# First taps of two depthwise convolutions on ScalarE, split loads, new orders, no identity products

## The reference, cut to what matters

```python
# block L0: window attention (8x8 windows, 4 heads), gated 1x1, dense 3x3 convolution
x = x + proj(attention(x))
h = w1 @ x + w1_b;  a, b = split(h)
g = a * sigmoid(b);  g = replicate_pad(g)
x = x + leaky(conv3x3(g, w2) + w2_b)
# block L1: linear attention with rope
x = x + dwconv(x, cpe1)                       # depthwise 3x3
y = ln2d(x);  act = silu(act_proj @ y);  y = in_proj @ y
t = silu(dwconv(y, dwc_w) + dwc_b)            # depthwise 3x3, nine taps
q, k = elu(qk_w @ t) + 1;  v = t
kv = sum_n rope(k) * v;  z = 1 / (q . mean(k))
attn = rope(q) @ kv * z + dwconv(v, lepe_w) + lepe_b   # depthwise 3x3, nine taps
x = x + out_proj @ (attn * act)
x = x + dwconv(x, cpe2)
x = x + fc2 @ gelu(fc1 @ ln2d(x))
```

## Time and profile before

| | |
|---|---|
| median of 3 runs | 798.58 us (796.69 to 803.7) |
| the profiled execution | 797.02 us, span of the core 795.0 us |
| mean granted TensorE clock | 0.959 |
| PE busy | 732.6 us, 92% of the span |
| DVE busy | 533.7 us, 67% |
| ACT busy | 450.0 us, 57% |
| POOL busy | 309.4 us, 39% |
| identity products (line 837) | 444 matmuls, 57.2 us |
| ACT table loads (line 1023) | 53, 68.0 us |
| DMA | 9% to 10% of the 16 engines' span |

### The profile page before, as it was taken

One profiled execution on the slowest core, in us unless ns is written; L12 is line 12 of the kernel. 1 busy time (PEld: TensorE's weight loads), 2 busy tenths in 40 slices (PEclk: granted clock), 3 DMA queues, 4 the chain that ended last, 5 costly groups with the idle time before them and its releaser, 6 DMA issues.

```text
span 795.0 us, 19684 instructions
## 1 busy us (share of the span) xinstructions
PE 732.6 (92%) x8424; PEld 463.3 (58%) x8424; DVE 533.7 (67%) x677; ACT 450.0 (57%) x638; POOL 309.4 (39%) x230
## 2 busy tenths in 40 slices
...
GB/s 60 33 68 16 2 31 2 2 2 15 1 16 17 32 31 31 16 32 1 31 31 46 21 27 2 2 2 31 32 16 1 27 22 16 1 31 1 43 5 45
...
## 3 DMA queue, kind: packets, MB, share of 16 engines
...
q10 hardware_dynamic: 512, 0.04, 0.1%
...
## 4 chain that ended last, share of the span: by engine, by line
PE 58%; DVE 22%; issue 6%; POOL 5%; ACT 4%; SPq 4%; DMA 1%; ACTq 0%; DVEq 0%; POOLq 0%
PE ps L590 21%; DVE QS L1178 9%; PE ps L580 7%; PE ps L681 5%; PE ps L837 4%; DVE CT L1192 3%; PE ps L656 3%; PE ps L667 3%; PE ps L765 2%; SPq L468 2%; PE ps L810 2%; PE ps L827 2%; DVE SC L1122 1%; PE ps L635 1%; PE ps L644 1%
## 5 line engine op out<-in xcount | busy, mean ns | idle before, releaser
L1331 POOL TENSOR_TENSOR SC<-SC,mx 128x768 f32<-128x768 f32 x48 | 77.2, 1609 | 172.5 <-DVE mx L1126 172.5
L590 PE MATMUL ps<-XP,wdw 48*64 48x384 f32 x1728 | 144.0, 483 | 0.0
L1192 DVE SCALAR_TENSOR_TENSOR CT<-TP,vec_sb,CT 112x768 f32<-112x768 f32 x96 | 123.6, 1304 | 1.3
L590 PEld LDWEIGHTS ps<-XP,wdw 48*64 48x64 f32 x1728 | 68.1, 132 | 69.4 <-issue 56.6
L1178 DVE SCALAR_TENSOR_TENSOR QS<-XP,vec_sb,QS 112x768 f32<-112x768 f32 x96 | 104.8, 1133 | 0.5
L1122 DVE TENSOR_TENSOR SC<-ps,bias_sb 128x768 f32<-128x768 f32 x48 | 45.7, 953 | 54.6 <-PE ps L656 54.1
L590 PE MATMUL ps<-G,w_sb 48*64 48x384 f32 x864 | 73.8, 493 | 1.3 <-ACT QH L1018 1.3
L681 PEld LDWEIGHTS ps<-vx,PT 128*128 128x128 f32 x576 | 66.6, 192 | 9.0 <-issue 5.5
L681 PE MATMUL ps<-vx,PT 128*128 128x52 f32 x576 | 68.8, 275 | 0.8 <-DVE XP L1152 0.4
L1023 ACT ACT_TABLE_LOAD x53 | 68.0, 1283 | 0.9
L1336 POOL TENSOR_TENSOR XP<-XP,YB 112x768 f32<-112x768 f32 x12 | 22.4, 1870 | 110.2 <-DMA YB<-YF 110.2
...
## 6 DMA issues: line engine op xcount, KB each, us to landing
XP<-in_x_dram SPq DMA_DIRECT2D x48, 72.0 KB, 2.5
YB<-YF SPq DMA_DIRECT2D x48, 72.0 KB, 2.2
XP<-XB SPq DMA_DIRECT2D x48, 72.0 KB, 2.4
...
wln_sb<-in_const_dram SPq DMA_DIRECT2D x6, 9.0 KB
```

What stands on the lines that cost most here:

```text
L590: mm = pe.matmul(slot(job)[half(c, HALF), r * BANK:r * BANK + SPX], w[half(r), tap * HALF:(tap + 1) * HALF], shifted(t, d * CROWS + c * WI ...
L1192: dve.scalar_tensor_tensor(out=ct, in0=win, scalar=wt, in1=ct, op0=ALU.mult, op1=ALU.add).then_inc(lepe_step, 1)
L1331: pool.tensor_tensor(sc, sc, bc_last(mx[:, (u % NSC) * 12:(u % NSC) * 12 + 12], TOK), ALU.subtract).then_inc(sub_ready, 1)
```

## The change

Six things change.

1. The first taps `c10` and `c20` of both depthwise convolutions (12 jobs each) leave VectorE. ScalarE computes them as Identity activations with scale and bias. Two new semaphores, dwc_begun and lepe_begun, hand them to tap 1 on VectorE.
2. The 37 loads of loaded_b are split. 24 stay, 13 (`wout`, `swap`, `wfc2`, the rope tables, the masks) get a semaphore of their own, loaded_c, and are issued last. Only DVE job `z0` waits for loaded_c. Strips 3, 4 and 5 of pair 0 are issued among and behind the 24.
3. `kp` computes km_sb with a SCALAR_TENSOR_TENSOR, of the head mask times the PSUM scalar times the head mask. The factor 1/PX that the TENSOR_SCALAR applied goes into a column of eye2_sb, by one small VectorE instruction in `s2`.
4. All `+n` marks are gone from PE_ORDER, so no identity product is left.
5. All five orders and the PSUM slots are new. Counted from the new ACT_ORDER, there are 48 table loads. Among the large moves: `f1` and `f2` of pair 1, chunks 1 and 2 go 75 to 77 places forward in PE_ORDER, with their `ge` on ScalarE 72 to 75 and `o.1.1`, `o.1.2` on VectorE 51 and 60 places. `s3.0.0` goes 37 places back on PE, `v.3.0` to `v.3.2` 32 to 43. On VectorE `z0.0.0` now stands behind `s2.0.0`.
6. `s2` on VectorE waits for the set-up of GpSimd.

```diff
 PE_ORDER = """
...
-    q.3.2@0 kp.3.0@3+21 kk.3.0@2+7 dn.3.0@0 dn.3.1@1 dn.3.2@3 at.3.0@2+23 at.3.1@0+6 at.3.2@2+12 op.3.0@1+4
-    op.3.1@0+4 d3.3.0@3+31 op.3.2@2 xc2.3.0@1+2 va2.3.0@0+4 f12.3.0@3+14 f11.3.0@2 d3.3.1@1 d3.3.2@0 xc2.3.1@3
-    f10.3.0@2 xc2.3.2@1 va2.3.1@0 f2.3.0@3 va2.3.2@2 f12.3.1@1+9 f11.3.1@3 f10.3.1@0 f2.3.1@2+12 f12.3.2@1
-    f11.3.2@3 f10.3.2@0 f2.3.2@2+6
...
+    kv.3.1@2 q.3.0@0 q.3.1@1 q.3.2@3 kv.3.2@2 kp.3.0@0 kk.3.0@1 dn.3.0@3 dn.3.1@2 dn.3.2@0 at.3.0@1 at.3.1@3
+    at.3.2@1 op.3.0@2 op.3.1@3 d3.3.0@0 op.3.2@1 xc2.3.0@2 va2.3.0@3 f12.3.0@0 f11.3.0@1 f10.3.0@2 d3.3.1@3
+    f2.3.0@0 xc2.3.1@2 d3.3.2@1 va2.3.1@3 xc2.3.2@0 va2.3.2@2 f12.3.1@1 f11.3.1@3 f10.3.1@0 f2.3.1@2 f11.3.2@3
+    f12.3.2@0 f10.3.2@1 f2.3.2@2
...
+def begun(text, prefix):
+
+    found = [(i, n) for name, i, n in jobs(text) if name == prefix]
+    return {t: j + 1 for j, t in enumerate(found)}
...
+DWC_BEGUN, LEPE_BEGUN = begun(ACT_ORDER, "c10"), begun(ACT_ORDER, "c20")
...
-        N_V, N_QK, N_A, N_W, N_B = 2, 8, 6, 8, 37
+        N_V, N_QK, N_A, N_W, N_B, N_C = 2, 8, 6, 8, 24, 13
...
-            for t in range(3, STRIPS):
-                load(0, t)
             for b in range(2):
                 img = slice(b * C, (b + 1) * C)
-                load_b(wout_sb[half(b), 0:C], wsq3[img, 9, img])
...
                 load_b(eye2_sb[half(b, C + 1), :], ident[0:C + 1, 0:HALF])
+                load(0, 3 + b)
...
             load_b(fc1b_sb[:, :], fc1b)
+            load(0, STRIPS - 1)
+            for b in range(2):
+                img = slice(b * C, (b + 1) * C)
+                load_c(wout_sb[half(b), 0:C], wsq3[img, 9, img])
...
+            load_c(masks_sb[:, :], masks)
+            load_c(rope_th_sb[:, :], rope_th)
+            load_c(rope_tw_sb[:, :], rope_tw)
...
+                elif name == "c10":
+                    wait_read(act, ("ip", i, halo_last(n)))
+                    if i:
+                        wait_filled(act, ("at", i - 1, n))
+                    act.activation(rows16(T0[n]), shifted(XP[i % 2], n * CROWS, CROWS, TAPS[0])[0:RG], ACT.Identity,
+                                   scale=v(f"dwc_{TAPS[0]}"), bias=v("dwc_b")).then_inc(dwc_begun, 1)
+                elif name == "c20":
+                    act.wait_ge(t_ready, i * CH + halo_last(n) + 1)
+                    if kc >= 2:
+                        wait_filled(act, ("op", (kc - 2) // CH, (kc - 2) % CH))
+                    act.activation(rows16(CT[kc % 2]), shifted(TP, n * CROWS, CROWS, TAPS[0])[0:RG], ACT.Identity,
+                                   scale=v(f"lepe_{TAPS[0]}"), bias=v("lepe_b")).then_inc(lepe_begun, 1)
...
                 if name == "z0":
-                    dve.wait_ge(loaded_b, N_B * 16)
+                    dve.wait_ge(loaded_c, N_C * 16)
...
+                    dve.wait_ge(setup_pool, N_POOL)
+                    dve.tensor_scalar(eye2_sb[:, C:C + 1], eye2_sb[:, C:C + 1], 1.0 / PX, None, ALU.mult)
...
-                    if k == 0:
-                        wait_read(dve, ("ip", i, halo_last(n)))
-                        if i:
-                            wait_filled(dve, ("at", i - 1, n))
-                        dve.tensor_scalar(rows16(T0[n]), win, wt, v("dwc_b"), ALU.mult, ALU.add)\
-                           .then_inc(dwc_step, 1)
+                    if k == 1:
+                        dve.wait_ge(dwc_begun, DWC_BEGUN[i, n])
...
-                        dve.tensor_scalar(km_sb[:, to], head_blocks[:, 0:C], slot(job)[0:RG, at:at + 1],
-                                          1.0 / PX, ALU.mult, ALU.mult)
+                        dve.scalar_tensor_tensor(out=km_sb[:, to], in0=head_blocks[:, 0:C],
+                                                 scalar=slot(job)[0:RG, at:at + 1], in1=head_blocks[:, 0:C],
+                                                 op0=ALU.mult, op1=ALU.mult)
```

More of the change, by code:

```diff
@@ new lines @@
+    vx.1.3 ex0.1.4 vx.1.4 sq.0.1 kx.1.5 ex1.1.4 rs.0.1 pt0.1.4 xw.1.5 pt1.1.4 sq.0.2 vx.1.5 ie.0.1 rs.0.2
+    ex0.1.5 c10.0.0 oe.1.2 ex1.1.5 ie.0.2 c10.0.1 sg.1.0 pt0.1.5 c10.0.2 ed.1.0 sg.1.1 oe.1.3 oe.1.4 ed.1.1
+    sg.1.2 pt1.1.5 ed.1.2 sg.1.3 ed.1.3 sg.1.4 ed.1.4 ts.0.0 yf.1.0 ve.0.0 oe.1.5 qe.0.0 ke.0.0 ts.0.1 yf.1.1
+    c20.0.0 sg.1.5 ve.0.1 ts.0.2 ed.1.5 ke.0.1 ar.0.0 c20.0.1 qe.0.1 yf.1.2 ve.0.2 ke.0.2 qe.0.2 x3.1.0 sq.1.0
+    ar.0.1 ar.0.2 rs.1.0 x3.1.1 ie.1.0 x3.1.2 z.0.0 z.0.1 sq.1.1 z.0.2 rs.1.1 sq.1.2 c20.0.2 ar.1.0 ie.1.1
```

266 lines of the change are left out of this document (129 added, 137 removed).

## The result

| | before | after |
|---|---|---|
| median, one chip | 801.14 us (796.69 to 807.52, 4 runs) | 778.02 us (772.93 to 780.43, 4 runs) |
| ratio | | 0.970, 95% interval 0.961 to 0.979 |
| profiled execution, span | 797.02 us, 795.0 us | 777.44 us, 775.6 us |
| mean granted clock | 0.959 | 0.940 |

The account below looks back on a forecast made before the run. TensorE and VectorE were taken to bound the kernel in turns, with a third regime in the tail from 700 us. Terms -6 - 8 - 4 - 2 + 0 + 0 = -20 gave 777.0, as a median 778.6 us; range 758 to 799.

Parts of the forecast that it names:

- load split: At the start: TensorE's wait for the last load and the low-clock stretch behind it go, -6.0 us (-6.8 to 0).
- first taps: 24 instructions leave VectorE for ScalarE, with 10.7 us of them on the chain: -8.0 us (-10.7 to 0).
- km_sb: In kp: the new instruction is only slowed by GpSimd, not made to wait for its end; -4.0 us (-5.3 to 0).
- products outside the tail: Two groups of four identity products before 100 us, where TensorE is full, are saved: -2.0 us (-4 to +4).
- tail: Last pair: about 5 us won without identity products, 5 lost to the low clock; 0.0 in sum (-5 to +9).
- new orders: All engines' job orders: nothing in the trace prices them, so 0, with 10 us either way.
- rival of the low clock: Tail, 744 us to the end: TensorE stays at 1.2 GHz, 34.6 us more, total 813 us; chance 0.11.
- rival of no relief: Taps wait for a late ScalarE or the clock falls there, so first taps give 0: 792 us; chance 0.19.
- signs that were named: Included no rope_tw wait before 42 us, full clock 42 to 50, idle under 35 us, d3.3.0 3 us earlier after kp.3.0.
- signs of error: Taps waiting over some tenths of a us, mean clock under 0.93, or TensorE idle growing beyond the identity products' time.

Follow-up runs that it names:

- b2: Kernel before with only the loads split and z0 behind s2 in VectorE's order: 798.05 us, ratio 0.997.
- a5: Changed kernel with the 37 table loads in one block again: 777.84 us, ratio 0.967 to the kernel before.
- b3: Kernel before with only the 24 first taps moved to ScalarE, other orders as they were: 801.94 us, ratio 1.0005.
- a2: Changed kernel with the 24 first taps back on VectorE: 792.46 us, ratio 0.990 to the kernel before.
- b5: Kernel before with split loads, first taps on ScalarE and the new km_sb form, but old orders and all identity products: 797.42 us, ratio 0.994.
- a3: Changed kernel with km_sb's instruction given one SBUF operand and one from PSUM: 777.47 us, ratio 0.973 to the kernel before.
- b6: b5 without its 67 identity products ahead of kk.3.0: 803.99 us, ratio 0.9996 to the kernel before.
- b1: Kernel before with only its 155 identity products from kp.3.0 on removed: 803.26 us, ratio 1.002.
- a1: Changed kernel with 100 identity products put back behind kp.3.0: 771.58 us, ratio 0.964 to the kernel before.

## Why the total was right and the terms were not

All measured parts stand beside the terms of the forecast. Ratios of separate parts are taken from different chips, so a us here is good to some 3 or 4.

| term | forecast | old orders | new orders |
|---|---|---|---|
| load split | -6 | -2, not told from 0 (b2) | 0 (a5), with the slow start |
| first taps | -8 | 0 (b3) | -14 to -16 (a2) |
| km_sb | -4 | within b5's -5 | 0 in the form used; 0 even at 0.2 us (a3) |
| products outside the tail | -2 | +4 to +7 (b5 to b6) | open: same slow start, not undone |
| tail | 0 | +2, not told from 0 (b1) | +8 |
| new orders | 0 | | the rest: with no taps moved, all else is -8 (a2) |

**The load split.** The wait and the clock loss were there, and b2 shows 4.4 us of them at `d0.0.0`. The gain was carried further than it looks from the ratio: 2.8 us at `kp.0.0` and at `kp.3.0`. Then one step at the low clock took 3.3 us. In the changed kernel the split itself does nothing, since TensorE reaches its first consumer about 6 us late for another reason, the missing products at the start.

**The first taps.** VectorE did lose the two lines, x12 each, and the others stayed at x96. No tap waited on the new semaphores but one, 0.7 us. The group of ScalarE's dwc taps in the changed kernel is 12.1 us, and with scale and bias one takes 1.02 us, where I had 0.90 from the row without a scale:

```profile
L1003 ACT ACTIVATE QS<-XP,vec_sb 112x768 f32<-112x768 f32 x12 | 12.1, 1023 | 0.1
...
L1202 DVE SCALAR_TENSOR_TENSOR QS<-XP,vec_sb,QS 112x768 f32<-112x768 f32 x96 | 100.6, 1092 | 1.1 <-ACT QS L1003 0.7
```

The sum over the chain's pieces, 10.7 us, was the wrong tool. With the old orders none of it came out at the end, and with the new ones more than all of it did (the bound was -10.7), though a2 also pays for an order that was made for taps on ScalarE. A piece of the chain has its price only if what stands behind it can move up. In b3 it did so in part (5.2 us at `kp.1.0`, 2.5 at `kp.2.0`, 3.1 at `kp.3.0`), and the clock behind `kp.3.0` took the rest.

**km_sb.** I read the SCALAR_TENSOR_TENSOR of line 1178, 1.01 us in the median and 2.55 at the most, as "only slowed", and so priced km_sb at 0.5 us. It measures 1.50 in the mean. The form change did nothing, as the rule from the Trainium skill (GPSIMD Engine Reference, section 8, Key points) had it: VectorE instructions with two SBUF inputs contend with GpSimd too. The traces of the changed kernel and of a1 agree: in the first pair the ends lie within 0.08 us of GpSimd's. The long instances of line 1178 wait too (the last section has them). The mistake was to take a median, set by the instances with no GpSimd work beside them, as evidence on those that had it. And even the real cure was worth nothing (a3), so the step failed twice: in the price of the new form, and in that anything there lay on the path. (TensorE idled for `kp` in all four pairs of the kernel before, for 2.4, 0.7, 3.5 and 2.9 us, not in pairs 0 and 2 alone. And 2 x 2 x 1.3 is 5.2.)

**Products outside the tail.** Priced as freed time. The prediction counted two groups of four ahead of 100 us and passed over the 14 products at `sc0.0.1` and the one at `av.0.0`. Those 14 were worth more as clock than as time: under the old orders their removal costs 5.9 us at `kp.0.0` (b5, b6), where the bound of the term was +4, and the changed kernel's trace shows the same slow start.

**The tail.** The forecast set a gain of 5 us against 5 of clock. The clock part was sized right for `d3.3.0`: 8.66 us against 6.04, plus 1.4 in `d3.3.1`. The 2.8 us of delay that leave with the products in front of `at.3.0` come back in part: `at.3.0` starts 10.0 us behind `kp.3.0` and not 11.2. So 1.2 us were won ahead of `d3.3.0` where 3.5 were forecast. What the forecast had not looked at was the order behind `d3.3.0`, which costs 5 to 6. The 8 us lie within the bound of +9.

The rival of the low clock named the right place and the right mechanism, at a quarter of its price: the mean from 686 to the end is 0.69 and not 0.50, since the convolutions brought the clock back each time.

**The new orders.** They were put at 0 for want of a row, with ±10 around it. They carry the gain. b5 has every other part and all the products and is at -0.6%, b6 without the products ahead of `kp.3.0` is at 0.0%; the changed kernel is at -3.0%, with the tail's +8 in it. Which of the moves in the orders pays is not known: no run moves one of them alone ahead of the last pair.

**The sum.** The terms ahead of the tail were forecast at -20 us and the profiles give -27.4. The tail was forecast at 0 and gives +8. That the two errors cancelled, and 778.6 was met, is luck. The rival of no relief leaves out the term of km_sb: with it, its 792 would be 788.

**The signs that were named.** Met: no wait on rope_tw, clock 1.00 from 42 to 50, the line counts. Missed: idle time under 35 us (43.3), km_sb at 0.2 to 0.5 us (0.9 to 1.8), `d3.3.0` 3 us earlier relative to `kp.3.0` (29.7 against 30.9). Of the signs of error none came up in the profile: no tap waits, the mean clock is 0.94 (0.928 in one other execution), and TensorE's idle time grew by 18.7 us (62.4 to 81.1), less than the 57.2 of the products.
